# A decoder layer on one Trainium2 core: attention in double-steps of eight self and eight cross heads

## What is computed

```python
x = layernorm(x + self_attention(x, w_q, w_k, w_v, w_o))      # 16 heads of 64, causal
x = layernorm(x + cross_attention(x, ctx, ctx, mask, ...))    # 16 heads of 16, biases
x = layernorm(x + moe(x, ...))   # twice: 32 experts of width 128, the best two of each token
```

## Time and profile before

| | |
|---|---|
| time, median of 3 runs | 4757.99 us (4751.04 to 4760.77) |
| the profiled execution | 4757.9 us, its span 4756.2 us |
| mean granted clock of TensorE | 0.992 |
| busy in the span | PE 4648.3 us (98%), weight loads 3981.4 (84%), DVE 3782.9 (80%), ACT 3412.8 (72%), POOL 2692.6 (57%) |
| first block | to about 3730 us; the first matmul of the second is at 3742.08 |
| the span in 40 equal slices | PE busy for 9 tenths or more in 36 of them; 8 in the first, the 31st and the last, 6 in the 32nd, where the blocks meet |

### The profile page before, as it was taken

The page is one execution under the profiler, slowest core; times in us unless marked ns, Lnnn a source line. Parts: engine busy times, 40 slices in busy tenths (PEclk is TensorE's granted clock), DMA queues, the critical chain, the costliest instruction groups (busy, mean ns, idle before and its releaser), DMA issues. The chain is left out here.

```text
span 4756.2 us, 133366 instructions
## 1 busy us (share of the span) xinstructions
PE 4648.3 (98%) x38848; PEld 3981.4 (84%) x38848; DVE 3782.9 (80%) x18827; ACT 3412.8 (72%) x13381; POOL 2692.6 (57%) x3748
## 2 busy tenths in 40 slices
PE   8999999999999999999999999999998699999998
PEld 7888888888888888888888888888887577878786
DVE  5888888888888888888888888888888356657888
ACT  5888887888888878878888878878877344444443
POOL 3455555555555555555555555555555455556777
PEclk9999999999999999999999999999999799999999
DMA  4221111211111211111111112111114499998998
GB/s 143 70 65 63 59 59 59 66 63 62 59 59 59 69 63 61 59 59 62 65 63 60 59 59 66 64 63 59 59 57 138 134 303 348 323 305 257 307 313 282
DMA packets 477441, 552.31 MB, mean 116 GB/s; under 512 B 55632, under 2 KB 408144, under 8 KB 476240
## 3 DMA queue, kind: packets, MB, share of 16 engines
q1 hardware_dynamic: 350800, 296.21, 19.8%
q0 software_dynamic: 52224, 146.87, 8.3%
q10 hardware_dynamic: 73728, 100.70, 6.9%
HBM read 266.21 MB, written 277.35 MB: 114 GB/s over the span
## 5 line engine op out<-in xcount | busy, mean ns | idle before, releaser
L534 POOL TENSOR_TENSOR yTl<-yT,yTh 128x256 fp32r<-128x256 f32 x512 | 382.7, 748 | 907.8 <-DVE yTh L991 904.7
L761 ACT ACTIVATE prob<-prob,negmax 128x128 f32<-128x128 f32 x2048 | 799.0, 396 | 103.6 <-DVE negmax L839 99.2
L761 ACT ACTIVATE xprob<-xprob,xnegmax 128x128 f32<-128x128 f32 x2048 | 792.5, 391 | 1.3 <-DVE xnegmax L839 1.3
L1165 POOL DMA_INDIRECT y_d<-y,to x576 | 564.4, 980 | 363.8 <-DVE y L1307 279.1
L1218 PE MATMUL bank<-moe,xgT 128*128 x2304 | 597.3, 382 | 4.4 <-issue 4.2
L593 POOL DMA_INDIRECT xs_d<-xrow,place x512 | 516.0, 1008 | 127.9 <-issue 127.6
L839 DVE CUSTOM_DVE_ANT_0 prob<-bank,causal 128x128 f32<-128x128 f32 x2048 | 471.5, 286 | 33.9 <-PE bank L699 20.5
L779 ACT COPY probT<-bank 128x512 f32<-128x512 f32 x512 | 300.6, 587 | 254.2 <-PE bank L709 185.1
L839 DVE CUSTOM_DVE_ANT_0 xprob<-bank,xmask 128x128 f32<-128x128 f32 x2048 | 470.5, 286 | 1.1 <-remote 1.1
L849 DVE TENSOR_TENSOR prob<-prob,inv 128x512 f32<-128x512 f32 x512 | 440.1, 860 | 20.2
L1218 PEld LDWEIGHTS bank<-moe,xgT 128*128 128x128 f32 x2304 | 394.4, 191 | 38.8 <-issue 8.5
(11 more groups left out here) (178 smaller groups left out, 14223.0 us busy)
## 6 DMA issues: line engine op xcount, KB each, us to landing
xg<-xs_d SPq DMA_DIRECT2D x576, 129.0 KB
xs_d<-blank SPq DMA_DIRECT2D x248, 272.0 KB
rows<-y_d ACTq DMA_DIRECT2D x256, 256.0 KB
xT_s<-xT SPq DMA_DIRECT2D x128, 128.0 KB
x<-x SPq DMA_DIRECT2D x128, 128.0 KB, 2.0
cT<-cT SPq DMA_DIRECT2D x128, 128.0 KB
x_d<-x SPq DMA_DIRECT2D x128, 128.0 KB, 2.0
sums<-x_d ACTq DMA_DIRECT2D x128, 128.0 KB
```

Of the source, the lines that this page charges most:

```text
L534: nc.gpsimd.tensor_tensor(yT_p[1][:, c, :], yT[:, c, :], yT_p[0][:, c, :].bitcast(F32), ALU.subtract).then_inc(y_split, 1)
L761: last = nc.scalar.activation(dst[:, h, :], dst[:, h, :], ACT.Exp, bias=src_bias[:, h:h + 1], scale=-1.0, accum_out=acc[:, h:h + 1])
L1165: nc.gpsimd.indirect_dma_start(y_d[:, :], bass.IndirectOffsetOnAxis(ap=to[:, m % NTO:m % NTO + 1].bitcast(U32), axis=0), y_s[q][:, :], Non ...
```

## The change

An iteration of four steps becomes two double-steps, numbered n from -4 to 2 x 128 + 13, each with eight self and eight cross heads. What is due in n is given by `AFTER` (batch b has its job in step 2b + AFTER) and the cross heads follow five double-steps behind the self heads. On every engine the order of an even and of an odd double-step is written out.
- PE: the transposes go into the score banks of their own attention, four heads ("a side") at a time, once DVE has masked that side. They stand among the projections. The cross heads' mix takes one of the three banks that go round (the job "xy"); every projection now has a whole bank.
- ACT: four query and key results instead of two; yT in one copy for eight heads, xyT in one.
- DVE: no yT and no query or key results. The norms are in different double-steps: the first in the odd, the second in the even, each with its own inverse root on POOL.
- POOL: also the high part of yT, both parts as operations of 128x512.
- x_s and mask_s have one buffer instead of two; two of the weights are staged through the buffer of the probabilities, so that the first masking waits for the split of wo.

The core of the diff (functions written anew stand with their new lines; the old ones are in the kernel above, and indentation is cut):

```diff
-GH = 4
-NG = H // GH
+GH = 8
+PH = GH // 2
-JOBS = [
-    (0, "qk0", -2, 0), (0, "qk1", -2, 0), (0, "xk", 1, 0),
-    (1, "o2", 3, 0), (1, "rank", 4, D), (1, "o1", 1, 0),
-    (2, "qk2", -2, 0), (2, "qk3", -2, 0), (2, "v0", -1, 0),
-    (3, "x1t", 1, 0), (3, "x2t", 3, D), (3, "v1", -1, 0), (3, "xq", 1, 0), (3, "route", 3, D), (3, "xv", 1, 0),
-]
+EVEN = ("qk0", "o2", "qk1", "x1t", "v1", "xq", "xv", "rank", "xy")
+ODD = ("qk2", "x2t", "qk3", "o1", "route", "xk", "v0", "xy")
 QK = ("qk0", "qk1", "qk2", "qk3")
+AFTER = dict(qk0=-4, qk1=-4, qk2=-3, qk3=-3, v0=-1, v1=0, o1=3, xk=3, x1t=4, xq=4, xv=4, o2=8, x2t=9, route=9, rank=10)
+CROSS = 5
...
-    prob = [sb(f"prob{p}", [P, GH, P]) for p in (0, 1)]
-    split_s = sb("split_s", [P, KC * HD])
+    prob = sb("prob", [P, 2, GH, P])
+    probT = sb("probT", [P, GH, P])
...
-    x_s = [sb(f"x{p}", [P, D]) for p in (0, 1)]
+    x_s = sb("x_s", [P, D])
-    mask_s = [sb(f"mask{p}", [P, P], I32) for p in (0, 1)]
+    mask_s = sb("mask_s", [P, P], I32)
-    yT, xyT = sb("yT", [P, PAIRS, P]), sb("xyT", [P, KC, P])
+    yT, xyT = sb("yT", [P, PH, P]), sb("xyT", [P, KC, P])
...
-    SC, T, XT, PV, JB = banks[0:2], banks[2], banks[3], banks[4], banks[5:8]
-    SELF, CROSS = slice(0, 2 * P), slice(2 * P, 3 * P)
+    SELF_BANKS, CROSS_BANKS, PV, JB = banks[0:2], banks[2:4], banks[4], banks[5:8]
     HALVES = (slice(0, P // 2), slice(P // 2, P))
-    SELF_SCORES = [SC[h % 2][:, h // 2 * P:(h // 2 + 1) * P] for h in range(GH)]
-    CROSS_SCORES = [SC[h // 2][:, (2 + h % 2) * P:(3 + h % 2) * P] for h in range(GH)]
...
-    return split_s[:, :]
+    return prob[:, :, :, :].rearrange("p s h k -> p (s h k)")
...
+        if b is not None:
+            wait(sp, xmask_ready, b)
+            sp.dma_start(mask_s[:, :], mask[bass.ds(b, 1), :, :].rearrange("o p n -> (o p) n")).then_inc(mask_in, 16)
+        b = due(n, 9, NB)
...
+    def split_y(m):
+        b, g = heads_of(m)
+        c = slice(g * PH, (g + 1) * PH)
+        pool.wait_ge(yT_in, m + 1)
+        if g == 0:
+            wait(pool, made["o1"], b)
+        nc.gpsimd.tensor_copy(yT_p[0][:, c, :], yT[:, :, :]).then_inc(y_high, 1)
+        pool.wait_ge(y_high, m + 1)
+        nc.gpsimd.tensor_tensor(yT_p[1][:, c, :], yT[:, :, :], yT_p[0][:, c, :].bitcast(F32), ALU.subtract).then_inc(y_split, 1)
...
+    def double_step(n):
+        if live(n - 2):
+            split_y(n - 2)
+        b = due(n, 4, NB)
+        if b is not None:
+            spread_keys(b)
+        b = due(n, 11, NB)
+        if b is not None:
+            open_blocks(b)
+        b = due(n, 12, NB)
+        if b is not None:
+            scatter(b, (0, 1))
+        if split_pair(n) is not None:
+            x_low(split_pair(n))
+        b = due(n, 8, NB)
+        if b is not None:
+            root(1, b)
+        b = due(n, 13, NB)
+        if b is not None:
+            scatter(b, (2, 3))
+        b = due(n, 4, NB)
+        if b is not None:
+            wait(pool, moved["o2"], b - 1)
+            pool.wait_ge(x1_ready, b + 1)
+            nc.gpsimd.tensor_tensor(x1b[b % 2][:, :], x1[b % 2][:, :], xbo_s[:, :], ALU.add).then_inc(x1b_ready, 1)
+        b = due(n, 10, NB)
+        if b is not None:
+            token_rows(b)
+        b = due(n, 3, NB)
+        if b is not None:
+            root(0, b)
...
+    def free_bank(n, name):
+        prior = bank_before(n, name, NB)
+        if prior:
+            wait(pe, xyT_in if prior[0] == "xy" else moved[prior[0]], prior[1])
...
+        wait(pe, maxed, 2 * n)
+        wait(pe, probT_in, 2 * (n - 1))
+        for pair in range(PH):
+            for side in (0, 1):
+                last = nc.tensor.matmul(SELF_BANKS[side][:, pair * P:(pair + 1) * P], qT[HALVES[side], b % 4, g * PH + pair, :],
+                                        kT[HALVES[side], key_slot(b), g * PH + pair, :], start=True, stop=True)
+        last.then_inc(scores, 1)
+    def cross_score(x):
...
+    def turn(n, side):
+        if not live(n - 1):
+            return
+        pe.wait_ge(normed, 2 * (n - 1) + side + 1)
+        if live(n):
+            pe.wait_ge(maxed, 2 * n + side + 1)
+        else:
+            wait(pe, probT_in, 2 * (n - 2) + side + 1)
+        for i in range(PH):
+            last = nc.tensor.transpose(SELF_BANKS[side][:, i * P:(i + 1) * P], prob[:, (n - 1) % 2, side * PH + i, :], ident[:, :])
+        last.then_inc(turned, 1)
...
+        if live(n):
+            score(n)
+        if live(n - CROSS):
+            cross_score(n - CROSS)
+        if n % 2 == 0:
+            job(n, "qk0")
+            turn(n, 0)
+            job(n, "o2")
+            turn(n, 1)
+            job(n, "qk1")
+            cross_turn(n, 0)
+            job(n, "x1t")
+            cross_turn(n, 1)
+            job(n, "v1")
+            job(n, "xq")
+            job(n, "xv")
+            job(n, "rank")
+        else:
+            job(n, "qk2")
+            turn(n, 0)
+            job(n, "x2t")
+            turn(n, 1)
+            job(n, "qk3")
+            cross_turn(n, 0)
+            job(n, "o1")
+            cross_turn(n, 1)
+            job(n, "route")
+            job(n, "xk")
+            job(n, "v0")
+        mix(n)
+        cross_mix(n)
...
+    def move_y(n):
+        y = n - 2
+        if live(y):
+            act.wait_ge(mixed, y + 1)
+            wait(act, y_split, y)
+            nc.scalar.copy(yT[:, :, :].rearrange("p c q -> p (c q)"), PV[:, :]).then_inc(yT_in, 1)
+        x = n - 2 - CROSS
+        if live(x):
+            act.wait_ge(xmixed, x + 1)
+            nc.scalar.copy(xyT[:, x % 2, :], jb(n - 1, "xy")[:, 0:P]).then_inc(xyT_in, 1)
...
+    def double_step(n):
+        move_y(n)
+        exponentials(n, 0)
+        move_turned(n, 0)
+        move_qk(n, "qk2" if n % 2 else "qk0")
+        exponentials(n, 1)
+        move_turned(n, 1)
+        move_qk(n, "qk3" if n % 2 else "qk1")
+        cross_exponentials(n, 0)
+        move_cross_turned(n, 0)
+        move_cross_turned(n, 1)
+        if n % 2 == 0:
+            move_v(n, "v1")
+        else:
+            move_xk(n)
+            move_v(n, "v0")
+        cross_exponentials(n, 1)
+        b = due(n, AFTER["route"], NB)
+        if b is not None:
+            act.wait_ge(moved["route"], b + 1)
+            nc.scalar.activation(soft[:, :], below[:, :], ACT.Exp).then_inc(soft_ready, 1)
...
+        if n == 0:
+            dve.wait_ge(*LOW_DONE[3])
+        dve.wait_ge(scores, n + 1)
+        wait(dve, turned, 2 * (n - 1))
+        for side in (0, 1):
+            four_masked(prob[:, n % 2, :, :], SELF_BANKS[side], causal, negmax[n % 2], side).then_inc(maxed, 1)
...
+    def even_step(n):
+        place_tokens(n)
+        masked(n)
+        cross_masked(n)
+        b2 = job_of(n, "o2")
+        if b2 is not None:
+            steps2 = residual(n, "o2", 1, norm2_step, sum2, x1b[b2 % 2], x1b_ready, b2 + 1)
+        normalise(n, 0)
+        if b2 is not None:
+            variance(steps2, 1)
+        weigh(n)
+        normalise(n, 1)
+        if b2 is not None:
+            dve.wait_ge(rsqrt_ready[1], b2 + 1)
+            wait(dve, x2_out[b2 % 2], b2 // 2 * 16)
+            wait(dve, xrow_ready, b2 - 1)
+            nc.vector.tensor_scalar(x2[b2 % 2][:, :], sum2[:, :], mv[:, 1, 0:1], rs[:, 1:2],
+                                    ALU.subtract, ALU.mult).then_inc(x2_ready, 1)
+        move_transposed(n, "x1t")
+        cross_normalise(n, 0)
+        b = job_of(n, "xq")
+        if b is not None:
+            dve.wait_ge(made["xq"], b + 1)
+            for m in range(KC):
+                last = nc.vector.tensor_scalar(xqT[b % 2][:, m, :], jb(n, "xq")[:, m * P:(m + 1) * P], xbq_s[:, m:m + 1],
+                                               XD ** -0.5, ALU.add, ALU.mult)
+            last.then_inc(moved["xq"], 1)
+            dve.wait_ge(mask_in, (b + 1) * 16)
+            nc.vector.tensor_scalar(xmask[b % 2][:, :], mask_s[:, :], 0.0, -BIG, ALU.is_equal, ALU.mult).then_inc(xmask_ready, 1)
+            dve.wait_ge(made["xv"], b + 1)
+            nc.vector.tensor_tensor(
+                xvD[b % 2][:, :, :].rearrange("p h (j d) -> p h j d", j=XHALF)[:, :, :, 0:XD],
+                jb(n, "xv")[:, 0:D].rearrange("p (h j d) -> p h j d", h=2 * KC, j=XHALF),
+                xbv_s[:, :].rearrange("p (h j d) -> p h j d", h=2 * KC, j=XHALF), ALU.add).then_inc(moved["xv"], 1)
+        cross_normalise(n, 1)
+    def odd_step(n):
+        rank_moves(n)
+        masked(n)
+        cross_masked(n)
+        normalise(n, 0)
+        move_transposed(n, "x2t")
+        if split_pair(n) is not None:
+            wait(dve, made["v1"], 2 * split_pair(n) - 2)
+            x_split_high(split_pair(n))
+        normalise(n, 1)
+        cross_normalise(n, 0)
+        b1 = job_of(n, "o1")
+        if b1 is not None:
+            steps1 = residual(n, "o1", 0, norm1_step, sum1, x_s, x_in, (b1 + 1) * 16)
+        top_two(n)
+        if b1 is not None:
+            variance(steps1, 0)
+        cross_normalise(n, 1)
```

(82 more changed lines are left out.)

633 lines of the change are left out of this document (235 added, 398 removed).

## The result

The changed kernel takes 5203.25 us (median of 4 runs, 5190.54 to 5205.27), the kernel before 4759.38 us beside it: a ratio of 1.0929, interval 1.0905 to 1.0953. The forecast was 4811 us, in 4690 to 4885: the sign was right, the size was not. The profiled execution has a span of 5203.4 us, 447.2 more than before, with PE busy 4658.9 us of it (90%), DVE 74%, ACT 63%, POOL 53%.

A forecast was written before the change was run, and what follows sets the result against it. PE's stream bounds the kernel before; after the change a circle through PE, ACT and DVE would: 16.37 + 12.20 + 0.33 = 28.90 us a batch against 28.48, 0.42 x 126 = 53 us, 4757.9 + 53 = 4811 us, range 4690 to 4885.

The forecast's parts named there:

- The PE stream: TensorE's own work in one attention batch, without waits: 27.56 us after the change, against a period of 28.48 before.
- surplus of the wider groups: Extra PE time where the array changes between 128 and 64 rows or columns: 0.46 us a step, 0.92 a batch saved.
- first rival: PE stays the bound: 4642 us, or 4705 with PE waiting half a microsecond; together 0.21.
- The circle: Closed chain through PE, ACT and DVE from xq to v0 and back to xq, forecast at 28.90 us a batch.
- PE's part: PE's stretch of the circle, from the start of xq to the end of v0: 16.37 us.
- the other part: From v0's end through ACT's copy and exponentials and DVE's chain to x1T's copy and xq: 12.20 us.
- the cancelling rival: Circle without any POOL meeting, about 28.45 us, so PE's gain and its waits cancel: 4750 to 4767 us, chance 0.12.
- The term for POOL: DVE product with two SBUF inputs slowed beside a POOL operation in the circle: 0.33 us, for one meeting.
- The third rival: POOL in the way: place_tokens' product and normalise 1 wait for whole POOL operations, 4934 us; 0.12 for 4885 and above.
- one wait at xq: Expected sign: PE waits once per batch, at xq on the x1T copy, 1 to 1.6 us.
- a wait on a masking: Sign against the forecast: PE waiting for transposes on a masking would mean the score banks, not x1T's copy, are the tie.
- The ramps: Start and end of the attention phase: bounded by -10 and +14 us, taken as 0.

The follow-up runs named there:

- both re-orderings: On the changed kernel, DVE copies x1T before normalising side 1 and ACT does the second four cross exponentials before moving xk and v0: 4630.85 us, 0.9752 of the kernel before.
- exponentials early: On the changed kernel, ACT does the second four cross exponentials of the odd step ahead of moving xk and v0: 4830.9 us, one run.
- `place_tokens` late: On the changed kernel, DVE's place_tokens comes behind the sixteen maskings of the even step instead of ahead of them: 5115.2 us, one run.
- 128x4 copy on ACT: On the changed kernel, the 128x4 copy in place_tokens goes from DVE to ACT in the odd step, behind the router's exponentials: 5037.59 us, one run.
- POOL narrow: On the changed kernel, POOL's split of yT, spread cross keys and scattered rows are one column wide, those computations left out: 4853.45 us, one run.
- x1T early: On the changed kernel, DVE copies x1T ahead of the normalisation of side 1 and x2 in the even step: 4891.54 us, one run.
- three re-orderings: On the changed kernel, x1T copied early, cross exponentials early and place_tokens behind the maskings: 4739.01 us, 0.9984 of the kernel before.
- three, the scatters last: On the kernel with three re-orderings, POOL issues the even step's two scatters last: 4632.03 us, 0.9759 of the kernel before.
- nothing of POOL: On the changed kernel, POOL's split of yT, spread keys, scattered rows, x1b and last key multiplication are one column wide, computations left out: 4748.55 us, one run.

## Why the prediction was wrong in size

**The PE stream: right.** The forecast had 27.56 us once the surplus of the wider groups is gone; with no waits left it is 27.49. The first rival's 4642 us for "PE stays the bound" is 4631 in the kernel with both re-orderings. The saving of the change is real, 1.00 us a batch (0.92 forecast). Counted from start to start, the scores take 3.90 us of a batch for 4.32 before, the mixes 3.80 for 4.10, the transposes of the self probabilities 1.58 for 1.97; the other groups together take 0.1 more. In time it is 116 us, the very number of the forecast, and that is luck: 1.00 x 127 would be 127, and a longer end of the phase takes part of it back. POOL's busy time, forecast at some 20 us a batch, is 16.5 (600 of 1000 us at 27.49); nothing hung on it.

**The circle: right, place for place.** 16.40 us for PE's part against 16.37 (its terms add up to 16.36). For the other part, without POOL, 28.50 less 16.40 is 12.10 against 12.20. The sum of single durations, 28.57, came out as 28.50. That is also the period of before, so that the cancelling rival, 4750 to 4767, is what the change would be without POOL: 4748.55 in one run, with the kernel before at 4747.69 beside it.

**The term for POOL: this step failed.** "I take 0.33, the row itself, for one meeting." The runs showed five meetings and 3.02 us in its place; with POOL's work left out, the period fell by 2.91. Two things were wrong in the term.

First, the row was misread. I set the product's 1.02 beside the 1.73 of a full wait and found it far from it. But the product began at 2021.75 and POOL's copy at 2021.19, to end at 2022.23: at the product's start 0.48 was left. A full wait for the rest and then the product alone is 0.48 + 0.69, less an overlap of 0.15, and that is the 1.02. The row did not lie between the two rules, it was a full wait. In the changed kernel four of the five meetings add up the same way, less 0.13 to 0.15, and all five end behind POOL's operation: both 128x4 operations and the 128x2 product by 0.02 to 0.03 us, x1 by 0.15, the large product by 0.55. Only x1, with 0.55 left and 0.41 alone, is shorter than that sum, by 0.26. The Trainium skill ("SBUF — State Buffer", Who interferes with whom) says that whichever issues first has the shared ports and the other is blocked fully; these rows agree. What a meeting costs goes by how much of POOL's operation is left, and not by its whole length.

Second, I let only large products of two SBUF inputs meet POOL, which left two candidates. Three of the five were short operations: the 128x4 copy, the 128x4 scaling and the 128x2 product, 0.16 or 0.17 us each alone and 1.25, 0.56 and 0.72 beside POOL; the fourth was x1, a scaling of 128x256. The same section of the Trainium skill names copies and scalings too as able to contend with GpSimd, under conditions on their operands; the prediction drew on its sentence about two inputs alone. Not held are the maskings, which read PSUM (0.28 beside POOL's multiplications, 2010.82 to 2012.3), x1T's copy out of PSUM (0.41 beside POOL's copy in the kernel with both re-orderings), and the reductions. One pair of rows doesn't fit and stays open: two products of 128x64 in `weigh`, with both inputs in SBUF, take their usual 0.21 and 0.19 at 2016.39 and 2016.64, beside POOL's root of 128x1 (2016.23 to 2016.80).

The third rival had the place ("its split of y beside place_tokens, x1b beside normalise 1") and the direction. Its 29.9 us was too low, first by its own words: a wait for all of the 1.29 and all of the 0.74 is 2.03 us and not 1.3, so 30.6 us; then because three more operations meet POOL. And with 0.12 it was held too unlikely: "both meetings must fall badly in every batch". They do: POOL's split of y is released by ACT's yT copy, at 2007.24 right behind the exponentials that release DVE, and its root and x1b by DVE's own variance. Here one queue (ACT's) or DVE itself starts both sides of each meeting, so it comes back in each period.

**The wait at the maskings.** The forecast had one wait at xq of 1 to 1.6 us, and called a wait on a masking a sign that the score banks are the tie. There are two waits, 1.37 and 2.10, but the inference was wrong: both are stops of the same circle. x1 and `place_tokens` stand ahead of the maskings, so what is late there shows first at the masks' readers. It went or shrank in the runs that shortened the chain above it, with the banks as they are (none with the exponentials early or with `place_tokens` late, some 0.2 with POOL's work narrow, 0.60 with the 128x4 copy on ACT), and stayed where only the part below was shortened. Each wait also costs some 0.23 us beyond its row: the period less the waits shown is 27.92 to 27.98 us in the kernels with two waits (27.94 here), 27.71 to 27.74 in four with one, 27.49 to 27.55 with none. Of this, 0.17 is how the row counts: idle time starts at the end of the matmul before, and without a wait the next would have started ahead of that end. (27.98 with POOL narrow shows that its second, unlisted wait is there.)

**The clock: a term that was missing.** The median period accounts for 2.92 x 127 = 371 us. In 41 stretches between 200 and 3500 us, 139.9 us in total, TensorE was granted half its clock, and the periods that hold one are longer, 33.0 or so; over the phase they add 74 us. Before there is none. The prediction had no term for it; what led to it is in the last section.

**The ramps: 0 in sum, as taken, by luck.** The first eight periods give back 27 us more than before (the circle is not closed yet in them), the last seven cost 6, the first score comes 2 later, and from the last self score to the first matmul of the experts it is 113.1 us for 93.2. That is +1, from terms that lie outside the bounds of -10 and +14 and cancel. The end is longer in all the kernels with double-steps (102 to 117); I have not tried what makes it so. All terms: 371 + 74 + 1 = 446 of 447.2.

## What to carry to other kernels

When two engines share a path into memory, a short operation can cost what is left of the other engine's operation, so look in the timeline of both at the start of each small operation of the critical chain, the 128x4 ones too. When the changed order closes a circle, find the operations that stand in it only by their place in a queue (here the copy of x1T behind a normalisation, and four exponentials behind a copy) and move these: two such moves turned +9.3% into -2.5%. Before moving one, follow the queue that it will release, since a meeting taken from one operation can land on the next.

## What was not expected of the hardware

TensorE's granted clock fell between its two levels (2.4 and 1.2 GHz) in the middle of a phase in which it is 89% busy. Of one such place, the wait and the stretch behind it (timeline; then the windows' columns of the earlier trace rows):

```profile
1952.94 1.13 PE L668 MATMUL bank<-x1T,xwq_s 128*128 128x128 f32 x8 [2.10 <-DVE x1T L1046]
1953.91 1.81 PE L668 MATMUL bank<-xwv_s,cT 128*128 128x256 f32 x4
```

```profile
1953.50:1954.00 0.50, 0.50 (x7) 0.50 (x6) 0.11 (x1) 0.50 (x5) 0.00 (x0) 1.00 0.00 0
1954.00:1957.40 3.40, 3.40 (x24) 2.75 (x24) 2.34 (x9) 0.50 (x4) 0.00 (x0) 0.50 0.12 39
```

PE was idle for 2.10 us, worked again for over a microsecond at full clock, and was then granted half of it; xv took 1.81 us where it takes 1.03. All 41 stretches of the changed kernel begin like this, 0.8 to 1.5 us behind a wait at xq. By kernel, with the waits of a period and the time at half clock between 200 and 3500 us:

| kernel | waits of a period, us | at half clock, us |
|---|---|---|
| changed | 1.37 and 2.10 | 139.9 |
| place_tokens late, alone | 3.04 | 129.7 |
| 128x4 copy on ACT | 0.60 and 2.10 | 23.9 |
| exponentials early | 1.33, some of 2.02 | 10.2 |
| POOL narrow | 1.43 and some 0.2 | 0 |
| x1T early | 1.39 and 0.27 | 0 |
| before | none | 0 |
| both re-orderings, alone or with the copy on ACT | none, one of 3.07 | 3.4 |
| three re-orderings | 0.66, one of 2.00 | 3.4 |
| three, the scatters last | none | 0 |
| nothing of POOL | 0.78 | 0 |

In these runs the two kernels that wait the most, 3.47 and 3.04 us in a period, pay a second time, in the clock. Every stretch at half clock in the table begins within the last 0.4 us of a wait of 2.0 us or more, or within 1.5 us behind it. None begins at the waits of 0.27 to 1.43 alone. But most waits of 2.10 have none: with the one of 0.60 ahead of them they give 24 us, and with one of 1.37 eight microseconds ahead of them 140. What decides between them I have not separated.
